# Five attention and recurrence stages in a software pipeline: PSUM operands on VectorE, small steps moved from GpSimd, extra identity products, new instruction orders

## The reference

```python
# layer 0
ln  = layernorm(x);  q, k, v = split(ln @ w_qkv + b_qkv)       # 16 heads of 16
x   = x + attention(q, k, v, mask_self)  @ w_ao + b_ao
ln  = layernorm(x);  q = ln @ w_q + b_q;  k, v = split(ctx @ w_kv + b_kv)
x   = x + attention(q, k, v, mask_cross) @ w_co + b_co
x   = x + gelu(layernorm(x) @ w1 + b1) @ w2 + b2
# attention: scores = scores * mask - 10000 * (1 - mask), softmax, times v
# layer 1
xn  = layernorm(x);  sx = token_shift(xn)
xxx = tanh((xn + sx * maa_x) @ maa_w1) @ maa_w2                # five mixes
x5  = xn + sx * (maa_stack + xxx)
w   = exp(-exp(time_decay + tanh(x5[1] @ decay_w1) @ decay_w2))
r, k, v, g = x5[3] @ Wr.T, x5[0] @ Wk.T, x5[2] @ Wv.T, silu(x5[4] @ Wg.T)
for t in tokens:                                               # 32 heads of 8
    a = outer(k[t], v[t]);  out[t] = r[t] @ (u * a + s);  s = a + w[t] * s
x   = x + groupnorm(out) * g @ Wo.T
xn2 = layernorm(x);  sx2 = token_shift(xn2)
x   = x + sigmoid((xn2 + sx2*fmr) @ Wr2.T) * (relu((xn2 + sx2*fmk) @ Wk2.T)**2 @ Wv2.T)
```

## Time and profile before

| | us |
|---|---|
| median of three runs | 743.11 |
| lowest and highest | 741.23, 743.57 |
| the profiled execution, its own time | 742.92 |
| its span in the profile | 741.1 |

### The profile page before, as it was taken

The page is one execution under the profiler, slowest core; times in us unless marked ns, Lnnn a source line. Parts: engine busy times, 40 slices in busy tenths (PEclk is TensorE's granted clock), DMA queues, the critical chain, the costliest instruction groups (busy, mean ns, idle before and its releaser), DMA issues. The chain is left out here.

```text
span 741.1 us, 16759 instructions
## 1 busy us (share of the span) xinstructions
PE 646.6 (87%) x5585; PEld 542.6 (73%) x5585; DVE 592.4 (80%) x1434; ACT 574.4 (78%) x2002; POOL 368.8 (50%) x537
## 2 busy tenths in 40 slices
PE   5578999999999999999999999999999988787254
PEld 4456787888888888888888888888888878675222
DVE  2476579899998989898989898998999877757541
ACT  2578989798989898989989898989898874743111
POOL 1153454656665656646464646556656454414121
PEclk9689999999999999999999999999999999989655
DMA  8900022221304050505040312223140504040400
GB/s 302 319 34 8 2 69 62 62 68 52 86 18 120 2 136 2 136 1 138 1 124 13 94 44 79 59 65 74 31 106 2 136 1 128 2 128 5 123 8 7
DMA packets 54844, 52.76 MB, mean 71 GB/s; under 512 B 6127, under 2 KB 49511, under 8 KB 54375
## 3 DMA queue, kind: packets, MB, share of 16 engines
q1 hardware_dynamic: 54758, 51.70, 25.0%
HBM read 30.72 MB, written 4.19 MB: 47 GB/s over the span
## 5 line engine op out<-in xcount | busy, mean ns | idle before, releaser
L1067 ACT ACTIVATE SC<-SC,NMX 128x128 f32<-128x128 f32 x512 | 198.8, 394 | 6.8 <-DVE NMX L822 6.5
L1067 ACT ACTIVATION_READ_ACCUMULATOR SC<-SC,NMX 128x1 f32 x512 | 99.1, 194 | 0.0
L557 PE MATMUL PS_T<-CST,SC 128*128 128x128 f32 x512 | 81.3, 283 | 15.8 <-ACT SC L1067 6.4
L822 DVE TENSOR_REDUCE NMX<-SC 128x4 f32<-128x512 f32 x128 | 85.0, 668 | 3.4 <-POOL SC L1239 3.1
L799 DVE TENSOR_TENSOR SC<-PS_S,MASK 128x512 f32<-128x512 f32 x128 | 82.8, 670 | 5.9 <-PE PS_S L539 5.9
L1075 ACT ACTIVATE PT<-PS_T 128x512 f32<-128x512 f32 x128 | 77.0, 601 | 11.2 <-PE PS_T L557 10.2
L557 PEld LDWEIGHTS PS_T<-CST,SC 128*128 128x128 f32 x512 | 59.2, 144 | 30.6 <-ACT SC L1067 16.2
L894 DVE TENSOR_TENSOR_SCAN SS<-W,AJ 128x1024 f32<-128x1024 f32 x32 | 73.2, 2286 | 2.5 <-DVE AJ L887 0.5
L469 PE MATMUL PS_B<-B_LT,W 128*128 128x128 f32 x512 | 67.7, 290 | 7.5 <-ACT B_LT L1023 7.4
L469 PEld LDWEIGHTS PS_B<-B_LT,W 128*128 128x128 f32 x512 | 63.6, 203 | 11.4 <-ACT B_LT L1023 11.0
L1289 POOL TENSOR_TENSOR SS<-SS,KR 128x1024 f32<-128x1024 f32 x16 | 37.8, 2364 | 55.9 <-DVE SS L894 55.9
(11 more groups left out here) (154 smaller groups left out, 1600.0 us busy)
## 6 DMA issues: line engine op xcount, KB each, us to landing
W<-EW SPq DMA_DIRECT2D x32, 512.0 KB, 4.7
V<-values_by_head SPq DMA_DIRECT2D x32, 512.0 KB, 5.5
W<-in_weights SPq DMA_DIRECT2D x1, 4160.0 KB, 19.5
ENC<-in_enc SPq DMA_DIRECT2D x16, 128.0 KB, 2.4
...
```

Of the source, the lines that this page charges most:

```text
L557: last = pe.transpose(PS_T[:, j * T:(j + 1) * T], SC[:, nr(b, a) % 2, g, j, :], ident)
L822: dve.tensor_reduce(NMX[:, nr(b, a) % 2, GH * g:GH * g + GH], SC[:, nr(b, a) % 2, g], AX_X, ALU.max, negate=True)\
L1067: last = act.activation(SC[:, nr(b, a) % 2, g, j, :], SC[:, nr(b, a) % 2, g, j, :], ACT.Exp, bias=NMX[:, nr(b, a) % 2, h:h + 1], accum_out ...
```

## The change

1. **PSUM operands on DVE.** For the pairs in `DVE_ADDS`, `a_mask` writes its result back into its bank of `PS_S` and `a_addmask` reads it there. The group norm's small tiles `GM`, `GV` and `GY` lie in `PS_D`. `d_affine` writes into `PS_D` in place of `YA`, and `d_gated` reads it there. PE's waits for a free bank follow (`scores_read`: `a_dadded` for the pairs in `DVE_ADDS`).
2. **Steps that leave POOL.** `d_norm` goes to DVE. `a_lessmask`, `d_first_states` and the copies into `PREV`, `XN` and `XM` go to ACT; the last two are now at the head of `b_scale` and `d_scale`.
3. **Fewer instructions on DVE.** `d_ruk` is one multiplication (u sits in the new `USEL`, which replaces the selector on PE); `d_own` is one.
4. **Extra products.** `warm` issues a number of identity products on PE ahead of a piece's wait, at 23 places in the first four and the last iterations (`KEEP_WARM`), 89 in all; from batch 3 on it first waits until all masks are done.
5. **The table first.** ACT begins with an Exp on one column, before it waits for the inputs.
6. **New orders** for all five engines, with other lags.

```diff
+KEEP_WARM = {
+    ('a_turn', 0, 0): 4, ('a_val', 0, 0): 2, ('a_prob_turn', (0, 0), 0): 8, ('a_prob_turn', (0, 1), 0): 4,
+    ('a_enc_turn', 0, 0): 3, ('a_scores', 1, 0): 2, ('a_prob_turn', (0, 2), 1): 2, ('a_prob_turn', (1, 2), 0): 2,
+    ('a_query', 1, 1): 2, ('b_turn', 0, 15): 3, ('b_turn', 1, 15): 6, ('d_out', 0, 14): 2, ('d_turn', 0, 14): 5,
+    ('d_keyrec', 0, 14): 14, ('d_val', 0, 14): 2, ('d_own', 0, 15): 2, ('d_read', 0, 15): 2,
+    ('d_oturn', 0, 15): 1, ('d_yturn', 0, 15): 10, ('d_out', 0, 15): 2, ('d_turn', 0, 15): 5,
+    ('d_keyrec', 0, 15): 4, ('d_val', 0, 15): 2}
...
 DVE_ORDER = [
+    ("d_own", 0, 5), ("b_streams", 1, 4), ("b_streams", 2, 4), ("a_mask", (0, 1), 1), ("a_inverse", 1, 3),
+    ("a_addmask", (0, 1), 1), ("d_output", 0, 5), ("a_moments", 1, 2), ("d_means", 0, 5), ("a_maxima", (0, 0), 1),
+    ("d_centre", 0, 5), ("a_maxima", (0, 1), 1), ("d_spread", 0, 5), ("a_normal", 1, 2), ("d_guess", 0, 5),
+    ("a_mask", (0, 2), 1), ("d_guess", 1, 5), ("a_context", 1, 3), ("d_guess", 2, 5), ("d_newton", (0, 0), 5),
+    ("d_newton", (0, 1), 5), ("a_mask", (0, 3), 1), ("d_newton", (0, 2), 5), ("d_newton", (1, 0), 5),
+    ("d_newton", (1, 1), 5), ("d_newton", (1, 2), 5), ("a_sum", 1, 3), ("d_newton", (2, 0), 5),
+    ("d_newton", (2, 1), 5), ("b_stats", 0, 3), ("d_newton", (2, 2), 5), ("b_moments", 0, 3), ("d_norm", 0, 5),
+    ("a_addmask", (0, 3), 1), ("a_maxima", (0, 2), 1), ("b_normal", 0, 3), ("a_stats", 0, 0), ("a_query", 1, 2),
+    ("a_moments", 0, 0), ("d_gated", 0, 5), ("b_gate", 0, 4), ("a_maxima", (0, 3), 1), ("a_mask", (1, 0), 2),
+    ("a_normal", 0, 0), ("d_sum", 0, 5), ("a_mask", (1, 1), 2), ("d_stats", 0, 5), ("d_moments", 0, 5),
+    ("a_maxima", (1, 0), 2), ("a_mask", (1, 2), 2), ("a_mask", (1, 3), 2), ("a_addmask", (1, 3), 2), ("d_ruk", 0, 4),
+    ("a_maxima", (1, 1), 2), ("a_maxima", (1, 2), 2), ("d_normal", 0, 5), ("d_outer", 0, 4), ("d_outer", 1, 4),
+    ("b_sum", 0, 3), ("b_stats", 1, 3), ("b_moments", 1, 3), ("d_mixed", 0, 5), ("a_inverse", 0, 1),
+    ("d_mixed", 1, 5), ("a_maxima", (1, 3), 2), ("b_normal", 1, 3), ("d_scan", 0, 4), ("a_context", 0, 1),
+    ("a_query", 0, 0), ("b_mixed", 0, 3), ("d_rstate", 0, 4), ("a_sum", 0, 1), ("d_scan", 1, 4), ("d_mixing", 0, 5),
+    ("a_stats", 1, 1), ("b_streams", 0, 3), ("a_mask", (0, 0), 0)]
...
 POOL_ORDER = [
+    ("b_addnorm", 0, 4), ("b_addnorm", 1, 4), ("a_addmask", (0, 0), 1), ("a_root", 1, 2), ("a_addmask", (0, 2), 1),
+    ("a_addbias", 0, 1), ("b_addnorm", 2, 4), ("a_addbias", 1, 2), ("d_final", 0, 6), ("b_root", 0, 3),
+    ("a_root", 0, 0), ("b_addbias", 0, 3), ("a_addmask", (1, 0), 2), ("a_addmask", (1, 1), 2),
+    ("a_addmask", (1, 2), 2), ("d_root", 0, 5), ("d_shift", 0, 5), ("b_root", 1, 3), ("b_shift", 0, 3),
+    ("d_rstate", 0, 4)]
...
+        GM, GV, GY = (PS_D[:, 512 - n * RH:512 - (n - 1) * RH] for n in (1, 2, 3))
...
+        def scores_read(pe, n, g):
+            if n >= 0:
+                b, a = turn_of(n)
+                if (a, g) in DVE_ADDS:
+                    pe.wait_ge(a_dadded, nth(DVE_ADDS, b, (a, g)))
+                else:
+                    pe.wait_ge(a_masked, 4 * n + g + 1)
...
+            def warm(name, arg, b):
+                n = KEEP_WARM[(name, arg, b)] if (name, arg, b) in KEEP_WARM else 0
+                if n and b > 2:
+                    pe.wait_ge(a_masked, 8 * B)
+                for _ in range(n):
+                    pe.matmul(PS_S[:, 0, 0, :] if b > 2 else PS_B[:, 0, 0:P], ident, ident, start=True, stop=True)
...
             def a_query(b, a):
+                warm("a_query", a, b)
...
-                pe.wait_ge(a_masked, 4 * nr(b, a))
+                scores_read(pe, nr(b, a) - 1, 3)
...
+            for t in range(CT):
+                last = dve.tensor_scalar(USEL[:, t, :], hsel, col("u", t), None, ALU.mult)
...
-                dve.tensor_tensor(SC[:, nr(b, a) % 2, g], PS_S[:, g], over_heads(mask), ALU.mult).then_inc(a_masked, 1)
+                masked = PS_S[:, g] if arg in DVE_ADDS else SC[:, nr(b, a) % 2, g]
+                dve.tensor_tensor(masked, PS_S[:, g], over_heads(mask), ALU.mult).then_inc(a_masked, 1)
...
-                for k in range(CT):
-                    last = dve.scalar_tensor_tensor(RK[:, k, :], KR[:, 1, k, :], col("u", k), KR[:, 0, k, :],
-                                                    ALU.mult, ALU.mult)
+                dve.tensor_tensor(RK[:, :, :], KR[:, 1], KR[:, 0], ALU.mult).then_inc(d_rk, 1)
...
+            def d_norm(b, _):
+                dve.wait_ge(d_gr, 12 * b + 12)
+                dve.tensor_tensor(heads(O[:, :]), heads(O[:, :]), over_tokens(GY[:, :], RH, RS), ALU.mult)\
+                    .then_inc(d_n, 1)
...
-                dve.scalar_tensor_tensor(YT[:, :, :], YA[:, :, :], 0.5, tiles(G[:, :]), ALU.mult, ALU.mult)\
+                dve.scalar_tensor_tensor(YT[:, :, :], tiles(PS_D[:, C:2 * C]), 0.5, tiles(G[:, :]), ALU.mult, ALU.mult)\
...
+            act.wait_ge(set_dve, 1)
+            act.activation(EARLY[:, :], EW[:, 0, 0:1], ACT.Exp).then_inc(set_act, 1)
             act.wait_ge(in_first, IN_FIRST)
...
+                act.activation(PREV[:, b, :, :], tiles(values)[:, :, 0:2], ACT.Copy).then_inc(a_prev, 1)
...
+                act.activation(MADD[:, b % 2, :], MASK[:, b, :], ACT.Copy, bias=-10000.0, scale=10000.0)\
+                    .then_inc(a_less, 1)
...
+                act.activation(XM[:, :, 0:1], PREV[:, b, :, 0:1], ACT.Copy)
                 turned(XM[:, :, 1:T + 1], PS_D[:, 0:C], "r2_w", "r2_b").then_inc(d_ln, 1)
```

187 lines of the change are left out of this document (83 added, 104 removed).

## The result

The changed kernel takes 700.42 us (median of four runs, 698.4 to 703.45) against 742.17 for the kernel before on the same chip (739.7 to 743.57): ratio 0.944, 95% interval 0.941 to 0.948. It is faster by 42 us. The forecast was 722.5 with a range from 708 to 744, so the direction was right and the size was wrong by 22 us, outside the range. The profiled execution took 699.4, its span is 697.3.

A forecast was written before the change was run, and what follows sets the result against it. Bound by a ring of waits between full engines (39.2 us per period), with latency chains in fill and tail. Middle -10, fill -4, tail -6.5 from 742.92 gave 722.4, forecast as 722.5, range 708 to 744.

The forecast's parts named there:

- I count zero: Middle, PSUM operands: less contention shortens POOL's additions but gives DVE nothing, and POOL is half idle; 0 us.
- three quarters of one gap: Middle: b_normal's 0.95 us wait on POOL's root goes; 0.7 us per period taken, -10 us over 14 periods.
- two thirds of DVE's idle time: Middle: the most the new order could gain, -2.0 us per period, -28 us in all.
- R4: Rival, middle: the order gives two thirds of DVE's idle time; 704.6 at the most, 709 as its middle; chance 0.08.
- Binding (a): Middle: PE's next a_query waits for DVE's mask addition, not the mask, about 0.6 us later; claimed covered.
- R2: Rival, middle: DVE's PSUM accesses have a price, 1.3 us per batch, order gains nothing; 751 us; chance 0.11.
- Bindings (b) and (c): Middle: first-column copies add 0.2 us before d_shift and b_shift; d_shift must fit between d_normal and d_mixed, with less DVE work.
- The price of a PSUM operand: DVE in the middle: reading and writing PSUM taken as free; bounds 1.3 us per batch either way.
- The fill: Start: early table -1.3, extra products and less blocking shorten it, set-up +0.2; -4 us, from 0 to -7.
- The tail: End: extra products keep the clock up, d_read starts earlier, d_norm on DVE; -6.5 us, from -1 to -10.
- R3: Rival, ends: extra products don't hold the clock, ends give only -2.5; 730.6 us; chance 0.09.
- 3 of the 9 us: Tail from 712.57 on: of 9 us a full clock would give back on PE, 3 counted as gained.

The follow-up runs named there:

- e14: Changed kernel's content in the old orders, without extra products and early table, with masks and additions of DVE_ADDS back in SBUF: 741.0 us, period 39.2.
- e7: Changed kernel with a_lessmask and d_first_states back on POOL instead of ACT: 700.7 us.
- e1: Kernel before with only the new orders of the five engines: 777.2 us, period 42.9.
- e4: Changed kernel with all operands that went to PSUM (masks, group norm's small tiles, YA) back in SBUF: 734.0 us.
- e13: Changed kernel with d_norm back on POOL and the last Newton step writing to SBUF: 702.9 us, period 37.6.
- e2: Changed kernel's content in the orders of the kernel before, without extra products and early table: 797.3 us, period 43.2.
- e6: Changed kernel with only the group norm's small tiles back in SBUF, masks staying in PSUM: 733.6 us.
- e8: Changed kernel without the early Exp on ACT that loads the table: 702.6 us.
- e16: Kernel before with the 89 extra products and the early Exp added, nothing else: 734.6 us.
- e3: Changed kernel without the 89 extra products on PE: 704.3 us.

## Why the prediction was wrong

**What bounds the kernel.** Right. A ring of 39.2, not an engine: e14 keeps 39.2 with 0.9 us more work on DVE and 0.5 more on ACT.

**Work added and removed.** Right in kind. DVE's three merged or moved operations took 0.39, 0.41 and 0.43, as priced. ACT's new work, bounded by 1.07 us, did not show: 35.5 busy after, 35.6 before, and e7 finds none of it on the path. POOL's busy time fell by 3.2 us per period, not 2.0: `d_shift`, 1.86 in the median before, now takes 0.61. `a_normal` "stays too" was wrong: 0.405 instead of 0.558, 0.3 us per period; the orders did it, for e1 has 0.407.

**The step that failed: "taking its SBUF operand away shortens POOL's additions and gives DVE nothing; ... I count zero".** By e4 this zero is 33.6 us. I looked at who loses in the kernel before, and there DVE's short operations are not the ones that lose, because POOL stands idle beside them (e14 agrees: in the old orders the group norm in PSUM brings nothing): the 4.61 us in front of `d_norm` were among my own rows. I had noted that `d_norm` leaves POOL, and read it only as a shorter queue; that POOL's freed time would be filled with additions of 1.27 us in the same stretch was not followed up. One of my rows did show DVE losing, `a_normal` with 0.558 against 0.41, and I only said that it stays. The zero is where the forecast of the middle went wrong: with the new orders, the moved steps and the merged instructions but these operands in SBUF (e4), the period is 40.0, longer than the 39.2 of the kernel before, and not 0.7 shorter. With the operands in PSUM it is 37.3. The new orders lay POOL's work beside DVE's chain, and the shorter ring rests on DVE not being held up there.

**The middle, -0.7 per period foretold, -1.95 measured.** The term of the sum that was mis-sized most: -10 foretold over 14 periods, -21.4 over eleven, and part of the -9.5 of the last four. The mechanism behind it failed too, and not only the size. I took three quarters of one gap that I could name. The gap went (`b_normal` idle 14.6 us in all before, 1.7 after), but it was worth 0 to 0.3 us per period: e14 closes it in the old orders, and the period stays at 39.2; e13 opens it again, 0.73 of the 0.95, and the period grows by 0.3. (In e14 `a_normal` is held up for 0.5 us more per period, so part of the gap may have moved there.) That the middle went the way I foretold is in this part luck. The new orders form another ring, and its length can't be had by taking gaps from the old one. My bound for it, two thirds of DVE's idle time, was the right place to look: R4 (704.6 to 709) was the nearest case and had 0.08. e1 and e2 say why one should be careful in both directions: the same orders and the same content, each alone, cost 35 and 55 us.

**Binding (a), the banks held longer.** That it is covered was right: in the kernel after PE waits 1.9 us in all for DVE's additions. The piece I named was not the one that pays where it isn't covered: I named `a_query`, and in e2 the waits stand at `a_enc_turn`, which writes bank 1. What it costs without the cover was not worked out, and it is the dearest item of all: 56 us, e2 against e14. That would have been a better mechanism for the slower rival than R2.

**Bindings (b) and (c).** No cost. `d_shift`, foretold as "still over 1.2 in the median", takes 0.612: the outer products end before it starts. DVE waits 0.17 us for it in most batches.

**The price of a PSUM operand.** Right. Reading: 0.188 (mean of the first Newton step, both kernels) and 0.684 against 0.679 (median of the addition). Writing, which no row of before showed: 0.690 against 0.682 for the mask, 0.187 against 0.189 for the last Newton step. R2 had no ground. The Trainium skill ("VectorE: DVE Perf Modes", section "The TRN2 errata — SBUF-src ops pay a fixed extra latency per instruction") gives 120 cycles for a PSUM source against 58, an estimate of 65 ns per instruction; these rows don't show it. By that row only a PSUM source costs more, so the estimate would hold for the 16 of the 22 that newly read PSUM, 1.0 us per batch, not 1.4. On who is held up, the Trainium skill ("SBUF — State Buffer", section "Who interferes with whom") says that issue order decides, and not the shape of the operation; e6 agrees: in each of the three pairs POOL's operation had started first (372.36 before 372.61), and DVE's, the shorter one, waited.

**The fill, -4 foretold, -10.2 measured.** The table (-1.3 foretold) is worth 2.2 by e8's time. The products did not shorten the four records of `a_val`, which still take 2.04; the 16 behind them take 2.28 where they took 3.43. That the clock made them slow is not shown: the granted clock is 1.00 there in both kernels. Table and products together are worth 1.2 in the old orders (e16, fill 135.7), and in the new ones what each brings in the fill is lost in the scatter of the fills (126.6 to 129.3). So most of the 10 us comes with the orders and the content: e1, the new orders alone, has a fill of 132.0. Which piece of them carries it was not tried.

**The tail, -6.5 foretold, -12.2 measured with the last four intervals.** The signs came true: `b_mlp1` of the last batch at 3.84 (under 4.5 foretold), clock 0.93. For the old orders the mechanism was right: there the products bring `b_mlp1` to 3.84, and R3 falls (e16). The size was low because I counted 3 of the 9 us that the clock takes in the last stretch and almost nothing of the intervals in front: e16 alone gets 9.4 there. In the new orders most of this is got without any product: e3 has 9.5 of the 12.2, and the same 3.84. The gains of products and orders overlap and don't add.
